# Two router norms moved from VectorE to ScalarE, with an addend from GpSimd, in an attention and mixture-of-experts kernel

## The reference, cut to what matters

```python
def _L0_ffn_ref(x, Wr1, br1, ln_scale, ln_bias, Wr2, br2, W1, b1, W2, b2):
    h = jnp.einsum('bsd,dk->bsk', x, Wr1) + br1          # 128 -> 64
    mu = jnp.mean(h, axis=-1, keepdims=True)
    var = jnp.mean((h - mu) ** 2, axis=-1, keepdims=True)
    h = (h - mu) * jax.lax.rsqrt(var + LN_EPS) * ln_scale + ln_bias
    h = gelu_kernel(h)
    router_logits = jnp.einsum('bsk,ke->bse', h, Wr2) + br2
    ...
x = x + _L0_attn_ref(_layernorm(x, axis=-1), ...)
x = x + _L0_ffn_ref(_layernorm(x, axis=-1), ...)
```

## Time and profile before

| | us |
|---|---|
| median of 3 runs | 1596.81 (1596.6 to 1601.74) |
| the profiled execution's own time | 1608.78 |
| its span, first to last instruction | 1607.0 |
| busy in the span: PE, DVE, ACT, POOL | 1470.8, 1343.3, 1079.9, 1113.2 |
| attention, batches 0 to 7 | about 75 to 1163 |
| tail | about 1163 to 1241 |
| experts | about 1241 to 1607 |
| mean granted clock of TensorE | 0.95 |

### The profile page before, as it was taken

One profiled execution on the slowest core, in us unless ns is written; L12 is line 12 of the kernel. 1 busy time (PEld: TensorE's weight loads), 2 busy tenths in 40 slices (PEclk: granted clock), 3 DMA queues, 4 the chain that ended last, 5 costly groups with the idle time before them and its releaser, 6 DMA issues. The chain is left out here.

```text
span 1607.0 us, 48047 instructions
## 1 busy us (share of the span) xinstructions
PE 1470.8 (92%) x11467; PEld 1087.9 (68%) x11468; DVE 1343.3 (84%) x5147; ACT 1079.9 (67%) x2267; POOL 1113.2 (69%) x2082
## 2 busy tenths in 40 slices
PE   4799999999999999999999999999930999999997
PEld 2466666666666666666666666656420999999997
DVE  6799999999989989989998998888343778888886
ACT  3167777776777777777777777766710777777775
POOL 3178778778867877876886787757743466676666
PEclk8599999999999999999999999999955999999998
DMA  6846545534644644553474455332163244343443
GB/s 169 235 111 184 130 122 169 160 103 135 180 107 122 189 137 115 167 163 107 115 204 118 113 170 162 86 94 72 36 185 93 42 56 57 53 55 53 57 54 46
DMA packets 129844, 189.92 MB, mean 118 GB/s; under 512 B 20184, under 2 KB 93272, under 8 KB 129616
## 3 DMA queue, kind: packets, MB, share of 16 engines
q1 hardware_dynamic: 104048, 167.23, 38.2%
q0 software_dynamic: 25568, 20.14, 8.2%
HBM read 104.04 MB, written 69.96 MB: 108 GB/s over the span
## 5 line engine op out<-in xcount | busy, mean ns | idle before, releaser
L1161 DVE CUSTOM_DVE_ANT_0 junk<-pA,mask 128x512 bf16<-128x512 f32 (+3 forms) x1536 | 777.6, 551 | 93.3 <-PE pA L723 56.6
L1053 ACT ACTIVATE prob<-pB 128x512 f32<-128x512 f32 x480 | 287.5, 599 | 227.5 <-PE pB L741 211.8
L1687 POOL DMA_INDIRECT out<-yb,dst x142 | 230.8, 1625 | 130.9 <-ACT yb L1765 75.1
L739 PE MATMUL pB<-QL,K 97*128 97x512 f32 (+3 forms) x768 | 314.4, 410 | 4.2 <-ACT prob L1053 2.6
L725 PE MATMUL pA<-K,QU 96*128 96x512 f32 (+3 forms) x768 | 277.9, 363 | 15.5 <-DMA K<-split_operands 9.5
L741 PE MATMUL pB<-QU,K 97*128 97x512 f32 (+3 forms) x768 | 288.6, 377 | 1.7 <-ACT prob L1053 1.3
L1055 ACT ACTIVATE prob<-pB 128x512 f32<-128x512 f32 x480 | 285.7, 595 | 2.0 <-PE pB L739 1.7
L723 PE MATMUL pA<-K,QL 96*128 96x512 f32 (+3 forms) x768 | 275.0, 360 | 0.3 <-DVE acc L1161 0.2
L756 PE MATMUL pC<-prob,vext 128*17 128x256 f32 x3408 | 263.0, 387 | 1.9 <-issue 1.4
L626 POOL TENSOR_SCALAR_AFFINE_SELECT prob<-prob 128x129 f32<-128x129 f32 (+1 forms) x448 | 146.0, 326 | 135.9 <-ACT prob L1055 130.6
L739 PEld LDWEIGHTS pB<-QL,K 97*128 97x128 f32 x768 | 146.2, 191 | 131.8 <-ACT prob L1055 65.9
(11 more groups left out here) (302 smaller groups left out, 2931.9 us busy)
## 6 DMA issues: line engine op xcount, KB each, us to landing
QL<-split_operands SPq DMA_DIRECT2D x64, 256.0 KB, 3.6
QU<-split_operands SPq DMA_DIRECT2D x64, 256.0 KB, 4.1
K<-split_operands SPq DMA_DIRECT2D x64, 256.0 KB, 4.7
xg<-routed_rows SPq DMA_DIRECT2D x75, 132.0 KB, 2.7
split_operands<-c_h SPq DMA_DIRECT2D x32, 256.0 KB, 5.5
split_operands<-c_l SPq DMA_DIRECT2D x32, 256.0 KB, 5.8
QL<-split_operands SPq DMA_DIRECT2D x64, 128.0 KB, 3.6
QU<-split_operands SPq DMA_DIRECT2D x64, 128.0 KB, 4.0
```

The source lines that it names most:

```text
L739: mm = pe.matmul(out, K[0:r, s, k], QL[0:r, s, q], start=True, stop=True)
L1053: act.activation(p[:, 0:HALF], pB[:, 0:HALF], ACT.Exp, scale=SCALE).then_inc(p_exp, 1)
L1161: ttr = v.tensor_tensor_reduce(out[:, cut], src[:, cut], mask[:, P * masked:P * (masked + blocks)], 1.0, -3.0e38, ALU.add, ALU.max, acc[:, ...
L1687: po.indirect_dma_start(dram["out"], bass.IndirectOffsetOnAxis(dst[k][:, a:a + 1], 0), yb[k][:, a, :], None, compute_op=ALU.add).then_inc( ...
```

## The change

Both normalizations move from DVE to ACT. ACT computes `scale * x + bias` with scale = rstd and bias = -(mean * rstd), per row. POOL's `root` makes that bias: after the two old operations it issues two more (a multiplication by the mean and one by -1), each behind a wait on its own previous result, so `rs_r` and `rs_h` become three planes. Two new semaphores, `rows_ready` and `hidden_ready`, count ACT's results; PE's transposes and the reload of `xres` on SP wait for these.

The places also shift. The first norm's eight operations go to (3, 1), (3, 2), (3, 3), (3, 4), two each; one small DVE operation on the slot column (L1232) stays on DVE, now `router_slots`. The second norm's go to (5, 2) and (5, 3), four each. PE's "fold" goes from (5, 3) to (5, 4), ACT's part of it from (5, 4) to (5, 5); the context transposition "context 4" goes from (5, 5) to (5, 6) on PE and from (5, 6) to (5, 7) on ACT. The tail does all eight operations of each norm on ACT, in order.

```diff
-                "row 5": ((4, 1),), "hidden": ((4, 3), (4, 5)), "context 3": ((4, 7),), "row 6": ((5, 0),), "fold": ((5, 3),), "context 4": ((5, 5),), "row 7": ((6, 0),),
+                "row 5": ((4, 1),), "hidden": ((4, 3), (4, 5)), "context 3": ((4, 7),), "row 6": ((5, 0),), "fold": ((5, 4),), "context 4": ((5, 6),), "row 7": ((6, 0),),
...
-        STATS_AT, AGGREGATE_AT, APPLY_AT, ROOT_AT = ((2, 1), (2, 4)), (2, 6), ((3, 0), (3, 1), (3, 3), (3, 4)), (2, 7)
-        HIDDEN_AT, HIDDEN_ROOT_AT, NORM_HIDDEN_AT = ((4, 6), (4, 7)), (4, 8), ((5, 1), (5, 2))
+        STATS_AT, AGGREGATE_AT, APPLY_AT, ROOT_AT = ((2, 1), (2, 4)), (2, 6), ((3, 1), (3, 2), (3, 3), (3, 4)), (2, 7)
+        HIDDEN_AT, HIDDEN_ROOT_AT, NORM_HIDDEN_AT = ((4, 6), (4, 7)), (4, 8), ((5, 2), (5, 3))
...
-                po.tensor_tensor(out[:, :], out[:, :], mhalf[:, :], ALU.pow).then_inc(r_rs, 1)
+                po.tensor_scalar(out[:, 0, :], var[:, :, 1], eps, None, ALU.add).then_inc(r_rs, 1)
+                po.wait_ge(r_rs, mine[0])
+                po.tensor_tensor(out[:, 0, :], out[:, 0, :], mhalf[:, :], ALU.pow).then_inc(r_rs, 1)
+                po.wait_ge(r_rs, mine[1])
+                po.tensor_tensor(out[:, 1, :], out[:, 0, :], var[:, :, 0], ALU.mult).then_inc(r_rs, 1)
+                po.wait_ge(set_pool, POOL_SET)
+                po.wait_ge(r_rs, mine[2])
+                po.tensor_scalar(out[:, 2, :], out[:, 1, :], -1.0, None, ALU.mult).then_inc(r_rs, 1)
...
-                pe.wait_ge(r_ln, b * RLN_N + RLN_STATS + 1 + 4 * (half + 1))
+                pe.wait_ge(rows_ready, b * NB + 4 * (half + 1))
...
-                pe.wait_ge(r_hid, b * RHID_N + RHID_N)
+                pe.wait_ge(hidden_ready, b * NB + NB)
...
+            def router_apply(b, ts):
+                if ts[0] == 0:
+                    act.wait_ge(copied_out, b * 32 + 32)
+                    act.wait_ge(r_rs, ROOT_N * b + 4)
+                for t in ts:
+                    act.activation(rows[:, t, 0:E], xres[:, t, :], ACT.Identity, bias=rs_r[:, 2, t:t + 1], scale=rs_r[:, 0, t:t + 1]).then_inc(rows_ready, 1)
+
+            def hidden_normalized(b, ts):
+                act.wait_ge(r_rs, ROOT_N * b + ROOT_N)
+                for t in ts:
+                    act.activation(hr[:, t, :], hr[:, t, :], ACT.Identity, bias=rs_h[:, 2, t:t + 1], scale=rs_h[:, 0, t:t + 1]).then_inc(hidden_ready, 1)
...
+            router_apply(B, range(NB))
...
+            hidden_normalized(B, range(NB))
...
-                for t in ts:
-                    v.scalar_tensor_tensor(rows[:, t, 0:E], xres[:, t, :], mv_r[:, t, 0:1], rs_r[:, t:t + 1].to_broadcast([P, E]), ALU.subtract, ALU.mult).then_inc(r_ln, 1)
+            def router_slots(b):
+
+                v.wait_ge(copied_out, b * 32 + 32)
+                v.scalar_tensor_tensor(rows[:, :, E], rows[:, :, E], float(S), rows[:, :, E], ALU.add, ALU.max).then_inc(r_ln, 1)
...
-            def hidden_normalized(b, ts):
-                v.wait_ge(r_rs, 4 * b + 4)
-                for t in ts:
-                    v.scalar_tensor_tensor(hr[:, t, :], hr[:, t, :], mv_h[:, t, 0:1], rs_h[:, t:t + 1].to_broadcast([P, RH]), ALU.subtract, ALU.mult).then_inc(r_hid, 1)
```

More of the change, by code:

```diff
@@ L133, in attention_phase @@
         sent, sent_to = sb("sent", [P, NB, ROW]), sb("sent_to", [P, NB, TOPK], U32)
-        st_r, mv_r, rs_r = sb("st_r", [P, NB, 6]), sb("mv_r", [P, NB, 2]), sb("rs_r", [P, NB])
-        st_h, mv_h, rs_h = sb("st_h", [P, NB, 6]), sb("mv_h", [P, NB, 2]), sb("rs_h", [P, NB])
+        st_r, mv_r, rs_r = sb("st_r", [P, NB, 6]), sb("mv_r", [P, NB, 2]), sb("rs_r", [P, 3, NB])
+        st_h, mv_h, rs_h = sb("st_h", [P, NB, 6]), sb("mv_h", [P, NB, 2]), sb("rs_h", [P, 3, NB])
         hT, hr = rp, sb("hr", [P, NB, RH])
@@ L169, in attention_phase @@
         r_ln, r_rs, r_hid = sem("router_rows"), sem("router_rstd"), sem("router_hidden")
+        rows_ready, hidden_ready = sem("router_rows_normalized"), sem("router_hidden_normalized")
         r_act, r_gelu, r_top, r_exp = sem("router_act"), sem("router_gelu"), sem("router_top"), sem("router_exp")
@@ L189, in attention_phase @@
         ACT_OUT = {"row 1": (0, 4), "turn 0": (1, 1), "turn 1": (1, 4), "row 2": (1, 4), "context 0": (1, 6), "row 3": (2, 4), "context 1": (2, 6),
-                   "rows 0": (3, 4), "rows 1": (3, 6), "context 2": (3, 8), "context 3": (4, 8), "row 6": (5, 1), "fold": (5, 4),
-                   "context 4": (5, 6), "row 7": (6, 1), "context 5": (6, 6), "context 6": (7, 6)}
+                   "rows 0": (3, 4), "rows 1": (3, 6), "context 2": (3, 8), "context 3": (4, 8), "row 6": (5, 1), "fold": (5, 5),
+                   "context 4": (5, 7), "row 7": (6, 1), "context 5": (6, 6), "context 6": (7, 6)}
         DVE_OUT = {"context 7": (0, 6), "out 0": (1, 6), "out 1": (2, 0), "row 4": (3, 2), "row 5": (4, 2), "hidden": (4, 6), "logits": (6, 4),
@@ L219, in attention_phase @@
         SCAT_N = 16 * len(SCATTER_AT)
[L220 to L221 removed]
+        RLN_N, RLN_STATS, ROOT_N = 2 * NB + 1, 2 * NB, 8
+        RHID_N, RTOP_N, RTOP_DLT, RPOS_N = 2 * NB, 2 * NB + 5, 2 * NB + 1, 8
         D_R, SET_R = 16 * 3, 16
@@ L556, in root @@
                 (var, out), eps = ((mv_r, rs_r), (mv_h, rs_h))[i], (LN_EPS, ROUTER_EPS)[i]
-                have, mine = known(po, (b * RLN_N + RLN_STATS, b * RHID_N + 2 * NB)[i]), known(po, 4 * b + 2 * i + 1)
+                have, mine = known(po, (b * RLN_N + RLN_STATS, b * RHID_N + 2 * NB)[i]), [known(po, ROOT_N * b + 4 * i + n) for n in (1, 2, 3)]
                 po.wait_ge(set_pool, POOL_SET)
                 po.wait_ge((r_ln, r_hid)[i], have)
-                po.tensor_scalar(out[:, :], var[:, :, 1], eps, None, ALU.add).then_inc(r_rs, 1)
-                po.wait_ge(r_rs, mine)
-                po.tensor_tensor(out[:, :], out[:, :], mhalf[:, :], ALU.pow).then_inc(r_rs, 1)
+                po.tensor_scalar(out[:, 0, :], var[:, :, 1], eps, None, ALU.add).then_inc(r_rs, 1)
[6 more added lines that the diff above has]
+                po.tensor_scalar(out[:, 2, :], out[:, 1, :], -1.0, None, ALU.mult).then_inc(r_rs, 1)
             def scatter(b, n):
@@ L1088, in batch @@
                             rows_kept(b + 1, KEEP_AT.index((h, u)))
+                        if (h, u) in APPLY_AT:
+                            router_apply(b, range(2 * APPLY_AT.index((h, u)), 2 * APPLY_AT.index((h, u)) + 2))
+                        if (h, u) in NORM_HIDDEN_AT:
+                            hidden_normalized(b, range(4 * NORM_HIDDEN_AT.index((h, u)), 4 * NORM_HIDDEN_AT.index((h, u)) + 4))
                         if (h, u) == TANH_AT:
@@ L1483, in _ @@
             router_aggregate(B)
-            router_apply(B, range(NB))
+            router_slots(B)
             v.wait_ge(m_ready, m_at(B, "hidden") + 1)
@@ L1488, in _ @@
             hidden_aggregate(B)
-            hidden_normalized(B, range(NB))
             cube(B)
```

17 lines of the change are left out of this document (4 added, 13 removed).

## The result

The change made the kernel slower: 1629.3 us in the median of four runs (1627.57 to 1630.86) against 1598.44 (1596.60 to 1601.74). That is 1.9% between the medians. The ratio on record is a little lower, 1.0159, and its 95% interval of 1.0129 to 1.0190 excludes 1 as well. I had forecast 1600.2 and a range of 1590 to 1611. The profiled executions stand at 1627.77 (span 1626.0) and 1608.78 (span 1607.0): +19.0.

The account below looks back on a forecast made before the run. It took a ring of PE, ACT and the `pB` halves to bound the kernel. Terms of -2.8, -2.3, +4.3, +0.7 and +3.5 gave +3.4 us on the median 1596.81: 1600.2 us, range 1590 to 1611.

Parts of the forecast that it names:

- The sum: Whole kernel: -2.8 head 5, -2.3 clock, +4.3 POOL's addend, +0.7 head 3, +3.5 tail, giving +3.4 us.
- Head 5 at full clock: Units (5, 1) to (5, 7): 13.31 us against 13.71, so -0.40 a batch, -2.8 in seven loop batches.
- (5, 4): PE has done its pair and fold while ACT normalized, so a bare unit: Head 5: PE works ahead during the normalizations, so unit (5, 4) lasts only 1.27 us.
- nothing absorbed: Rival, 8%: PE can't work ahead of late ACT; (5, 4) and (5, 6) last 2.16 plus transposes; 1617 us.
- Batch 7 in head 5: The last batch, without a first pass for PE, was counted as no change.
- The clock: Behind PE's gap at (5, 3): four clock falls of seven at 1.4 us, 5.6 against 7.9, so -2.3.
- ACT's operations: Each 64-column normalization on ACT: 0.34 us from start to start, 0.44 long.
- POOL's addend: Unit (3, 1): 0.68 us added behind POOL's power, 0.13 given back; net 0.55 a batch, +4.3 in all.
- ACT in head 3: Units (3, 2) to (3, 5): 7.76 us against 7.66, +0.1 a batch, +0.7 in seven batches.
- DVE's relief: DVE loses 16 operations a batch, 3.8 us; counted as no gain.
- The tail: After the last batch, both norms on ACT with POOL's addends lengthen the chain by 3.5 us.
- the last two cases and a quarter of the first: Slower outcomes: clock rival (17%, 1606 to 1611 us), nothing absorbed (8%), and a quarter of the forecast case (55%).

Follow-up runs that it names:

- copy first: The changed kernel with ACT's context copy of head 4 issued ahead of the four normalizations in (5, 3); median 17.2 us below the changed kernel's, 7.0 at equal clock.
- the 22 waits: The changed kernel with 22 already satisfied waits added on DVE at (5, 3); medians 1.9 us below the changed kernel, 5.0 at equal clock.
- copy first and 22 waits: The changed kernel with ACT's context copy ahead of the normalizations in (5, 3) and 22 satisfied DVE waits; median 1615.4 us, +6.4 at equal clock.
- addend split off: As copy first and 22 waits, with only POOL's two addend operations of the first norm moved to (2, 8), behind the mask; +7.2 us at equal clock.
- second norm only: The changed kernel with the first norm back on DVE without addend, context copy early, 11 DVE waits; medians show no difference from before, -2.3 us at equal clock.

## Why the prediction was wrong, point by point

The sum said +3.4 us for the profiled execution, and +19.0 was measured. The step that failed is the unit after the norms in head 5, and beside it stand a term that was missing, a batch that I had put at nothing, and an assumption on the clock.

- **Head 5 at full clock, wrong: -0.40 a batch, measured +0.8** (14.55 from (5, 1) to (5, 8) in a batch without a fall, against 13.71). The step that failed is "(5, 4): PE has done its pair and fold while ACT normalized, so a bare unit". It lasted 2.18 and not 1.27. I had asked what ACT waits for and what fold waits for, and not what the *pair* waits for. I even counted the context copy at its new place behind the normalizations, as 0.29 of ACT's time, and did not ask who needs its result. With the copy first the unit is 1.18, and head 5 comes to -0.13; the rest of my -0.40 went as (5, 5) to (5, 7) took 0.1 to 0.2 longer each than I had put them. The 8% rival "nothing absorbed" named one right symptom, (5, 4) at 2.16, for another reason; its other one, (5, 6) at 2.16, measured 1.53.
- **DVE's back edge, missing.** +7.0 in head 0, the largest single item beside head 5, has no row in the kernel before and no term in my sum. I counted added operations engine by engine, and never weighed that removed instructions may cost.
- **Batch 7 in head 5, put at nothing, measured +2.3.** It has the same late copy, and a fall behind it. With the copy first it was 0.1 shorter than before.
- **The clock: right in the trace, wrong for the median.** In the seven batches of the loop there were four falls, as taken; they lengthened head 5 by 5.0 in all against my 5.6. But I had carried the 12 us between the profile of the kernel before and its median over, as if the changed kernel's median would run at the better clock too. Its four runs had 0.949 to 0.951: these 12 us are what the medians show beyond the traces. Whether the change itself lowers the clock of typical runs isn't settled; the same kernel before had 0.943 to 0.957 in its 47 runs.
- **ACT's operations, right.** 0.33 from start to start and 0.43 long for 64 columns (four in 1.43) against my 0.34 and 0.44. The Trainium skill, "ScalarE: Activation LUTs", section "What ACT_TABLE_LOAD costs", had 0.33 by the sum that I made of it, and is the closer by 0.01.
- **POOL's addend, right:** +0.54 for +0.55, with the 0.13 given back by L639. Two experiments show that at two other places of POOL's operations it isn't dodged: off PE's path it is on ACT's.
- **ACT in head 3, right** (+0.10 for +0.1 beside the addend, head 3 in all +0.65).
- **DVE's relief at nothing, wrong as a principle, small in size.** The places moved without it buy nothing (13.69), as DVE's lag takes fold's place at (5, 4). With it, and with the copy first, they buy 0.13 a batch. I had counted the moved places' gain and the relief's gain of zero as two items; they are one.
- **The tail, right:** +3.5 to fold for +3.5; 1.0 came back behind it.
- **The chances,** a slip in the sum: the last two cases and a quarter of the first make 0.39 for "slower", and not 0.37, which leaves 0.41 for "within".

At equal clock my terms gave +5.7. The kernel with the two missed causes taken out measured +6.4, the changed kernel +19.4. So the forecast failed by what a late copy holds up, by an edge that no row showed, and by one assumption on the clock. Its sizes for ACT, POOL and the tail held.

## What to carry to other kernels

When an operation is put ahead of another in an engine's order, list what it pushes back and who waits for *that*. Here eight operations cost head 5 nothing with the copy of 0.4 us ahead of them (13.58 against 13.71), and 0.8 a batch with the copy behind them. Compare two kernels at the same mean granted clock before explaining microseconds, and then look at their clocks too: of the 17 us that the copy brought, 10 were there. Look at the loop's back edge on each engine whose instruction count changes. Spread moved work over units in which the engine has idle time of its own: here this shortened the chain by 0.3 a batch and the other engine's gap from 0.86 to 0.51.

## What the runs showed of the hardware

- The same loop with 875 recorded instructions a round idled DVE for 1.4 to 1.9 us at its back edge and with 878, 882, 886 or 902 for 0.45 (0.43 in the kernel before, with 892, and with 903). Removing instructions from an engine that isn't the bound made the kernel 5 us slower by this, the gain of the 22 waits at equal clock.
- PE waited 0.84 to 0.87 us (0.95 to 0.98 in batch 7) for head 5's late exponential. With this as the only long wait there, the clock fell to half in 0 (copy first), 2 (copy first and 22 waits), 4 (addend split off) and 4 (second norm only) of 8 batches; with a second wait of 0.95 behind it in 5 (the changed kernel). A wait of 0.51 to 0.53 (0.62 in batch 7) was followed by a fall in none of 8. The same program shows both outcomes in successive batches, and what decides between them stays open.
- Most such falls took 3.4 us and lengthened head 5 by some 1.5; with 22 waits alone one took 23.9 us and, over heads 5 and 6, 9.9.
- Over 47 runs of one unchanged program, the time ran from 1600.8 to 1620.6 us and nearly all of that went with the mean granted clock (0.957 to 0.943; correlation -0.97).
